# AdaLN block on one core: the routing stage in another order, one-hot tables as a step of their own

## What is computed

```python
mod = (silu(c) @ wmod).reshape(4, 6, 1, 512)       # sa, ca, ga, sb, cb, gb
h = layernorm(x) * (1 + ca) + sa
x = x + ga * attention(h)                          # 16 heads of 32, rope, causal
h = layernorm(x) * (1 + cb) + sb
# routed feed-forward on h: 128 old experts, 48 kept, 8 per token of 512
logits = where(old_to_new == -1, -inf, h @ gate_weight.T)
top_v, top_i = top_k(softmax(logits), 8); top_v /= sum(top_v)
pos = running position of each (token, expert) in its expert's list; kept if pos < 192
x = x + gb * sum over the kept experts of w * down(silu(g) * u)
```

## Time and profile before

| | |
|---|---|
| median of 3 runs | 4234.07 us (4231.8 to 4234.41) |
| the profiled execution | 4235.04 us, of which the span of its instructions 4233.2 us |
| granted clock of PE, mean | 0.948 |
| busy, share of the span | PE 91%, DVE 65%, POOL 66%, ACT 43% |
| the four routing stages together | 506.6 us, mean of one 126.6 us |

### The profile page before, as it was taken

How to read it: one execution, slowest core, us unless ns; L and a number is a source line. 1 busy time by engine, 2 the same in 40 slices (tenths; PEclk the granted TensorE clock), 3 DMA queues, 4 the chain that set the end, 5 groups by cost and what they waited for, 6 DMA issues and landing times. The chain is left out here.

```text
span 4233.2 us, 81098 instructions
## 1 busy us (share of the span) xinstructions
PE 3848.5 (91%) x21344; PEld 2333.0 (55%) x21344; DVE 2753.7 (65%) x5889; ACT 1805.8 (43%) x3526; POOL 2774.7 (66%) x2251
## 2 busy tenths in 40 slices
PE   5989999987999999879899999879899999859998
PEld 2755554456744554457655554457555544547776
DVE  3767677466757767476667776567676774646655
ACT  1345655423355555332355555233455554311111
POOL 3768788824678878616578888427687887115554
PEclk8989999998999999989899999889899999979999
DMA  6543334252533343434433333425333332349997
GB/s 209 177 127 89 94 101 107 80 185 99 179 92 102 87 112 87 133 124 146 143 92 102 99 100 111 153 83 181 116 91 91 101 106 87 102 137 259 257 258 188
DMA packets 305135, 549.12 MB, mean 130 GB/s; under 512 B 59572, under 2 KB 99636, under 8 KB 301492
## 3 DMA queue, kind: packets, MB, share of 16 engines
q1 hardware_dynamic: 283192, 485.62, 38.3%
q0 software_dynamic: 21504, 58.40, 5.9%
HBM read 311.86 MB, written 174.85 MB: 115 GB/s over the span
## 5 line engine op out<-in xcount | busy, mean ns | idle before, releaser
L1141 ACT ACTIVATE Pt<-PS 128x512 f32<-128x512 f32 (+3 forms) x2560 | 1205.4, 544 | 1005.5 <-PE PS L1334 558.5
L1006 POOL TENSOR_TENSOR Sm<-Pt 128x512 f32<-128x512 f32 (+3 forms) x960 | 1027.7, 1077 | 356.2 <-ACT Pt L1141 337.9
L1653 DVE TENSOR_REDUCE part<-PS 128x1 f32<-128x512 f32 x1536 | 997.4, 684 | 295.9 <-PE PS L1311 291.6
L1311 PE MATMUL PS<-QK 96*128 96x512 f32 (+3 forms) x2560 | 1017.1, 418 | 56.7 <-DVE part L1649 23.9
L1334 PE MATMUL PS<-QK 97*128 97x512 f32 (+3 forms) x2560 | 991.9, 408 | 41.1 <-DMA QK<-mT 18.6
L1358 PE MATMUL PS<-Pt,V 128*32 128x512 f32 (+3 forms) x5120 | 874.0, 554 | 44.7 <-POOL Sm L1006 44.2
L1362 PE MATMUL PS<-Sm,onesv 128*32 128x512 f32 (+3 forms) x1920 | 822.6, 534 | 0.0
L1334 PEld LDWEIGHTS PS<-QK 97*128 97x128 f32 x2560 | 485.9, 193 | 481.9 <-issue 328.5
L1006 POOL TENSOR_TENSOR Sm<-Sm,Pt 128x512 f32<-128x512 f32 (+1 forms) x640 | 712.6, 1113 | 50.2
L1649 DVE CUSTOM_DVE_ANT_0 PS<-PS,consts 128x128 f32<-128x128 f32 (+3 forms) x1024 | 502.4, 495 | 346.8 <-PE PS L1311 344.0
L1311 PEld LDWEIGHTS PS<-QK 96*128 96x128 f32 x2560 | 496.6, 195 | 245.4 <-DVE part L1653 120.1
(11 more groups left out here) (169 smaller groups left out, 4907.9 us busy)
## 6 DMA issues: line engine op xcount, KB each, us to landing
QK<-qkd SPq DMA_DIRECT2D x720, 128.0 KB, 3.1
qkd<-st SPq DMA_DIRECT2D x64, 1024.0 KB, 4.5
Wg<-wgu SPq DMA_DIRECT2D x48, 768.0 KB, 4.9
o<-od SPq DMA_DIRECT2D x448, 64.0 KB, 2.0
W<-wd SPq DMA_DIRECT2D x3, 6144.0 KB, 21.6
Wd<-wdn SPq DMA_DIRECT2D x48, 384.0 KB, 5.8
xin<-x SPq DMA_DIRECT2D x16, 1024.0 KB, 7.8
vd<-vst SPq DMA_DIRECT2D x16, 1024.0 KB, 6.2
```

The source lines that it names most:

```text
L1006: nc.gpsimd.tensor_tensor(total, of[0][:, first:CH] if i == 1 else total, of[i][:, first:CH], ALU.add).then_inc(sum_done, 1)
L1141: nc.scalar.activation(Pt[:, t % NPT, first:CH], S2[t % NS2][:, first:CH], ACT.Exp, scale=SCALE).then_inc(exp_done, 1)
L1311: mm(s1[:, 0:w], QK[0:3 * HD, hh % 2, 0, qb * P:(qb + 1) * P], QK[0:3 * HD, hh % 2, 1, c * CH:c * CH + w], start=True, stop=True).then_inc ...
L1653: v.reduce_max(part[:, qb, cc:cc + 1], s1[:, 0:w], AX.X).then_inc(s1_dve, 1)
```

## The change

`routing()` returns another list, and the tables leave `place` for a step of their own, `spot`, in two halves. No arithmetic is added or removed.

```diff
+OUT_EARLY = {0: [(2, 0)], 1: [(2, 2), (2, 3)], 2: [(3, 2), (3, 3)]}
+OUT_AMID = {0: [(2, 1)], 1: [(3, 0)]}
+OUT_LATE = {1: [(3, 1)]}
 def routing():
-    out = [("join", NG - 1, NCH - 1)]
+    out = [("stat", 1)] + [("join", NG - 1, NCH - 1)] + turns(0, range(KT))
+    out += [("inverse", NG - 1, NCH - 1, i) for i in range(TPC)] + [("scale", NG - 1, NCH - 1), ("norm", 1), ("widen", 2), ("widen", 3), ("logit", 0)]
     for j in range(NCH):
         more = j + 1 < NCH
-        if j and more:
-            out += [("out", j + 1, 0), ("out", j + 1, 1)]
-        out += [("turn", j, ct) for ct in range(KT)] + [("logit", j)]
+        out += [("back", j, 0), ("back", j, 1), ("gate", j), ("back", j, 2), ("back", j, 3)]
+        out += outs(OUT_EARLY, j)
+        if 0 < j and more:
+            out.append(("stat", j + 1))
+        if j:
+            out.append(("spot", j - 1, 0))
+        if 0 < j and more:
+            out.append(("norm", j + 1))
+        if j:
+            out.append(("spot", j - 1, 1))
+        out += [("old", j, 0), ("old", j, 1)] + outs(OUT_AMID, j) + [("new", j)]
+        if j == 0:
+            out += turns(1, (0, 1))
+        out.append(("place", j))
         if j:
             out.append(("slot", j - 1))
-        else:
-            out += [("inverse", NG - 1, NCH - 1, i) for i in range(TPC)] + [("scale", NG - 1, NCH - 1), ("widen", 2)]
-        out.append(("gate", j))
-        if j and more:
-            out += [("out", j + 1, 2), ("out", j + 1, 3)]
-        if more:
-            out.append(("stat", j + 1))
-        if j == 0:
-            out.append(("widen", 3))
-        out += [("back", j, t) for t in range(TPC)] + [("old", j, 0), ("old", j, 1)]
-        if j == NCH - 1:
+        out += outs(OUT_LATE, j)
+        if j == 1:
             out.append(("lead_stat", j))
-        out.append(("new", j))
-        if j == NCH - 1:
+        if j == 2:
             out.append(("lead_xhat", j))
         if more:
-            out.append(("norm", j + 1))
-        out.append(("place", j))
-    return out + [("lead", NCH - 1), ("slot", NCH - 1)]
+            out += turns(j + 1, (2, 3) if j == 0 else range(KT)) + [("logit", j + 1)]
+    return out + [("lead", NCH - 1), ("spot", NCH - 1, 0), ("spot", NCH - 1, 1), ("slot", NCH - 1)]
...
-                    dve.wait_ge(r_ps, ONE + ci)
+                def spots(j, half):
+                    ci = NCH * b + j
+                    if half == 0:
+                        dve.wait_ge(r_ps, ONE + ci)
...
```

More of the change, by code:

```diff
@@ L236, in taken_by, with turns, outs @@
     return [use for use in FIRST if use[0] != "vproj"].index(step) + 1
+OUT_EARLY = {0: [(2, 0)], 1: [(2, 2), (2, 3)], 2: [(3, 2), (3, 3)]}
+OUT_AMID = {0: [(2, 1)], 1: [(3, 0)]}
+OUT_LATE = {1: [(3, 1)]}
 def routing():
-    out = [("join", NG - 1, NCH - 1)]
+    def turns(j, some):
+        return [("turn", j, ct) for ct in some]
+    def outs(at, j):
+        return [("out", *of) for of in at.get(j, [])]
+    out = [("stat", 1)] + [("join", NG - 1, NCH - 1)] + turns(0, range(KT))
+    out += [("inverse", NG - 1, NCH - 1, i) for i in range(TPC)] + [("scale", NG - 1, NCH - 1), ("norm", 1), ("widen", 2), ("widen", 3), ("logit", 0)]
@@ L1748, in positions @@
-                    dve.wait_ge(ab_ready, ONE + 2 * ci + 2)
-                    cp.link(v.tensor_scalar(tcol[:, :], tcol[:, :], float(TPC), None, ALU.add))
-                    cp.end()
+                    own = slice(half * TPC // 2, (half + 1) * TPC // 2)
+                    v.tensor_tensor(Aoh[:, own].rearrange("p t g a e -> p (t g) a e"),
+                                    hib[:, own, :].rearrange("p t (g e) -> p (t g) e", e=8).unsqueeze(2).broadcast_to([P, 6 * TPC // 2, 16, 8]),
+                                    table_of, ALU.is_equal)
@@ new lines, in spots @@
+                    cp.link(v.tensor_tensor(B1[:, own].rearrange("p t g (a e) -> p (t g) a e", e=8),
+                                            lob[:, own, :].rearrange("p t (g e) -> p (t g) e", e=8).unsqueeze(2).broadcast_to([P, 6 * TPC // 2, 16, 8]),
+                                            table_of, ALU.is_equal))
+                    v.tensor_scalar(B2[:, own, :, 0, :].rearrange("p t g c -> p (t g) c"), B1[:, own].rearrange("p t g c -> p (t g) c"), K[:, K_P1:K_P1 + 1], None, ALU.mult)
@@ L1752, in collect @@
+                    for t in range(own.start, own.stop):
+                        last = v.tensor_scalar(B2[:, t, :, 1, :], B1[:, t, :, :], tcol[:, t:t + 1], None, ALU.mult)
+                    last.then_inc(ab_ready, 1)
+                    if half == 1:
+                        dve.wait_ge(ab_ready, ONE + 2 * ci + 2)
+                        cp.link(v.tensor_scalar(tcol[:, :], tcol[:, :], float(TPC), None, ALU.add))
+                        cp.end()
                 def collect(j):
@@ L1783, in _ @@
                         positions(j)
+                    elif kind == "spot":
+                        spots(j, step[2])
                     elif kind == "slot":
```

## The result

The changed kernel takes **4285.99 us** (median of 4 runs, 4284.36 to 4287.53) beside 4234.24 us for the kernel before, a ratio of 1.0121 with a 95% interval of 1.0104 to 1.0139: slower by 1.2%. The forecast was 4283.

The account below looks back on a forecast made before the run. A dependency chain, no full engine, bounds the routing stages. Three batches of 6.2 plus 7.7 clock, a last of 1.6 plus 4.3, and 1.6 for tables beside POOL add 49.2 us: 4283 us; 8-in-10 range 4248 to 4312.

Parts of the forecast that it names:

- C: Interval from `key` of chunk 1 to `key` of chunk 2: 41.8 us in place of 32.6, +9.2; 35.2 in the last batch.
- D: Interval from `key` of chunk 2 to `key` of chunk 3: 31.8 us in place of 27.7, +4.1 at full clock.
- B: Interval from `key` of chunk 0 to `key` of chunk 1: 20.0 us in place of 28.7, -8.7.
- since only POOL's join and the weights' load wait a microsecond longer: Reason given that `key` of chunk 0 stays where it is when chunk 1's `stat` and `norm` move to the start.
- are what is gone from this path: Claim that moving the tables behind the next gate shortens the path from chunk 0's `key` to chunk 1's, -8.7 us.
- reason (1), the landing: Chunk 1: copies into `h2` wait for chunk 0's store, landing at 34.8 us; masked `ex` at 9.4 instead of 6.2.
- Issuing that store earlier does not help: Chunk 0's `h2` store: SP's queue held it for 10.58 us, with the DMA share at 1.0 behind 6 MB of weights.
- reason (3), the shift behind half of the tables: Chunk 1, DVE: the shift waits 3.06 + 0.2 us behind half tables; ACT then normalises before copying the gates out.
- E: Interval from `key` of chunk 3 to the stage's end: 32.2 us in place of 30.6, +1.6; 28.2 in the last batch.
- The clock term: PE at half rate behind idle gaps in chunks 1 and 2: 7.7 us a batch, 4.3 in the last.
- Half tables beside POOL: DVE's half tables run beside POOL's 1.02 us power at two places a batch: 0.2 us a place, 1.6 in all.
- DVE as the bound: Rival: PE's tiles and normalisation slip into time DVE needs anyway; a batch changes by -21.4, 4149 us; chance 0.06.

Follow-up runs that it names:

- b_split: Kernel before, with only tables in their own step behind the next chunk's gate and `slot` behind the next chunk's positions; 4278.03 us, ratio 1.0111.
- a_widen_wait: Changed kernel, but POOL's bias addition to chunk 3 waits until chunk 0's gates are masked; 4285.65 us, 1.0113 against the kernel before.
- a_widen_store: Changed kernel with POOL's chunk 3 addition held until chunk 0's gates are masked, and chunk 0's h2 store issued ahead of the weights; 4257.06 us.
- a_old_first: Changed kernel, but ACT copies the gates out ahead of the next chunk's normalisation in chunks 1 and 2; 4269.44 us, 1.0075 against the kernel before.
- a_slot2: Changed kernel with POOL's addition delayed, store early, gates copied before normalisation, tables moved into DVE's waits, chunk 2's `slot` beside chunk 3's gate, tile (3,1) before `slot`; 4177.36 us.

## Why the prediction was right, and where not

- **The total and the sign**: right. The reasons named in C and D hold, but the sum came out only because the error in B and the hidden wait in C cancel. The orders of ACT and DVE make D 34.4 (forecast 31.8 and 2.8 of the clock); undoing them gives 25.7.
- **B, -8.7**: measured -2.7. The step that failed is "since only POOL's join and the weights' load wait a microsecond longer". I had counted what waits behind the moved `stat` 1, and not what its power had been holding back on POOL's queue. With the addition out of the gate B is 21.3, against 20.0 laid out. The sentence that the tables "are what is gone from this path" was wrong as well: b_split takes the tables out of B, and B is 28.8 there. In the earlier trace rows DVE had been idle 3.44 us ahead of that `key`, so that the tables were not on the path. The new list also normalises chunk 1 early and leaves one tile less ahead of `key`; that these two shorten B fits, but no run took them apart.
- **C, reason (1), the landing**: right in mechanism and size, but the late gate hid it in two of the first three batches; it showed as soon as B was short (46.2 against 46.7). So the two errors cancelled in the first three batches, +13.0 against +13.9 each. That they work against each other is no accident: the landing comes at its time whenever `key` is ready (34.8 us into the first stage in the changed kernel, 35.0 in a_widen_wait), so that what B loses is not waited for in C, and a_widen_wait, with the short B, took 4285.65 us. That they cancel to within 1 us is luck. "Issuing that store earlier does not help" holds only behind the weights: ahead of them, in a_widen_store, it saved 28.6 us against a_widen_wait. The last batch, which has no such wait, could not cancel: +16.1 against +5.9.
- **C, reason (3), the shift behind half of the tables**: right as a stretch of the path (3.12 us from the aggregates to the shift, 3.26 laid out), mis-sized as a loss. POOL takes the power in that time, so the shift loses 1.8 us by it. The other half, ahead of `gN`, was not in the sum of C and D, and in the changed kernel it holds nothing: DVE is idle 3.15 us behind it, and `gN` of chunk 2 waits for PE. It counts once ACT's order is lifted (a_old_first).
- **E, +1.6**: measured +3.1, and in the last batch +6.1 against 3.8. The sum had `slot` of chunk 2 end with the positions, at full clock; it took 4.51 us at the low one, and the last tables waited 2.08 us for it.
- **The clock term**: about right in its sum, in another place: the tiles of C ran at full clock, since there was no landing to wait for; `slot` paid in C, D and E, 5.4 us together in the first batch over the 2.78 of the earlier trace rows, and in B the tile behind the gate, 1.5 us. These make about 6.9 of the 7.7 laid in; an estimate, since not every group is counted.
- **Half tables beside POOL**: the power took 1.65 and 1.66 us instead of 1.02, and the tables their usual 0.95. It cost nothing, since the shift stands behind the tables anyway. As in the earlier trace rows, who had started first kept its time. The Trainium skill (SBUF — State Buffer, "Who interferes with whom") has this as its rule, and the trace agrees; the same rule, read for the large addition, would have given the 4.62 us of `rep`.
- **The signs it had named**: the landing near 35 us into the stage (34.8), `gT` right behind `xn`, and stages of about 140 us (142.7, 140.5 and 140.8) came; the `key` of chunk 1 near 28 us (36.8) and a C over 40 did not, the exponential was held by the landing in the third batch only, and the last stage took 137.5 us, not 128.
- **The rivals**: DVE as the bound was not reached by any order tried; a_slot2 comes nearest, with 91 of 118 us.

## What to carry to other kernels

A step moved forward on one queue also lets go whatever stood behind it on the others: list for each engine what now starts earlier, and beside what it will run. Work that only fills time belongs where its engine waits anyway (here the tables ahead of the next `key`, `slot` beside a gate); in between a gate and its users it is on the chain. Where two queues each hold up the same result, lifting one gains little: both together gained 54.5 us, the two alone 16.6 and 10.7.

## What the runs showed of the hardware

An addition of 4.5 us on POOL stretched DVE's `tensor_scalar` on 128x512 from 0.43 to 4.62 us in the first batch of the changed kernel, until the addition was through. In the second batch it stretched one to 3.15 us, while the four match-and-replace instructions beside it kept their 0.28. A 1 MB store that waits behind 6 MB of loads held SP's queue for 10.54 us and landed after 22.0 (a_widen_wait); issued ahead of them it held the queue for 0.41 and landed after 5.3 (a_widen_store).
